# Causal attention: the first group's row maxima computed in two query halves

## The reference, cut to what matters

```python
qkv = (_ln(x, g1, be1) @ w_qkv + b_qkv).reshape(b, t, 3, h, dh)
...
k = jnp.concatenate([k_self, k_ctx], axis=1)
v = jnp.concatenate([v_self, v_ctx], axis=1)
scores = jnp.einsum('bthd,bshd->bhts', q, k) * scale
mask = (j >= t) | (j <= i)
scores = jnp.where(mask, scores, -jnp.inf)
attn = jax.nn.softmax(scores, axis=-1)
attn_out = jnp.einsum('bhts,bshd->bthd', attn, v).reshape(b, t, d)
```

## Time and profile before

| | us |
|---|---|
| median of 3 runs | 1572.62 (1569.34 to 1581.99) |
| the profiled execution, its own time | 1575.25 |
| its span | 1573.5 |
| stage `at0` in that span | about 80 to 429 |

### The profile page before, as it was taken

One profiled execution on the slowest core, in us unless ns is written; L12 is line 12 of the kernel. 1 busy time (PEld: TensorE's weight loads), 2 busy tenths in 40 slices (PEclk: granted clock), 3 DMA queues, 4 the chain that ended last, 5 costly groups with the idle time before them and its releaser, 6 DMA issues.

```text
span 1573.5 us, 21716 instructions
## 1 busy us (share of the span) xinstructions
PE 1345.9 (86%) x7242; PEld 767.7 (49%) x7242; DVE 1071.8 (68%) x2665; ACT 748.6 (48%) x1048; POOL 531.0 (34%) x448
## 2 busy tenths in 40 slices
PE   5869998999779979788998988799998688788896
PEld 4413333333268856544443355444443577545796
DVE  4577777777564367666577768675668888676654
ACT  5405555555867445522334434323343634245664
POOL 3001111111241043205777622078765357001312
PEclk9959999999999999988999989799999979699999
DMA  7952333330000001554313305724400030730001
GB/s 254 264 114 47 58 58 57 58 58 2 14 14 1 1 1 42 157 165 94 79 35 76 113 17 165 212 62 94 95 28 1 27 35 22 161 64 3 1 1 54
DMA packets 79848, 110.29 MB, mean 70 GB/s; under 512 B 16575, under 2 KB 55673, under 8 KB 77945
## 3 DMA queue, kind: packets, MB, share of 16 engines
q1 hardware_dynamic: 79737, 108.91, 27.9%
HBM read 70.55 MB, written 37.80 MB: 69 GB/s over the span
## 4 chain that ended last, share of the span: by engine, by line
PE 42%; DVE 18%; POOLq 15%; issue 10%; ACT 6%; DVEq 3%; DMA 3%; SPq 2%; POOL 1%; ACTq 0%
POOLq L1080 15%; PE banks L1191 6%; PE banks L1551 5%; PE banks L1133 5%; PE banks L1536 5%; PE banks L2096 3%; DVE max_parts L1365 3%; PE banks L1166 3%; PE banks L2122 2%; DVE mask_rows L1361 2%; DVE scratch L1361 2%; PE banks L1144 1%; PE banks L2640 1%; DMA stacks<-neg_max_parts 1%; PE banks L571 1%
## 5 line engine op out<-in xcount | busy, mean ns | idle before, releaser
L1326 ACT ACTIVATE x_feat<-banks,key_bias 128x1024 f32<-128x1024 f32 x160 | 176.5, 1114 | 268.4 <-PE banks L1173 210.4
L1079 POOL TENSOR_TENSOR x_feat<-x_feat 128x1024 f32<-128x1024 f32 (+1 forms) x112 | 243.0, 2170 | 98.7 <-ACT x_feat L1326 90.7
L1133 PE MATMUL banks<-stacks 128*128 128x512 f32 (+4 forms) x640 | 230.6, 408 | 39.9 <-DVE max_parts L1354 14.4
L1191 PE MATMUL banks<-x_feat,v_group 128*32 128x512 f32 (+4 forms) x1312 | 231.6, 570 | 8.7 <-ACT x_feat L1326 4.8
L1326 ACT ACTIVATE x_feat<-banks 128x1024 f32<-128x1024 f32 (+2 forms) x224 | 178.9, 840 | 121.9 <-PE banks L1166 120.1
L1133 PEld LDWEIGHTS banks<-stacks 96*128 96x128 bf16 (+1 forms) x640 | 77.7, 139 | 230.7 <-DVE max_parts L1354 92.9
L1166 PE MATMUL banks<-stacks 99*128 99x512 bf16 (+3 forms) x512 | 132.8, 348 | 23.5 <-ACT x_feat L1326 13.3
L1103 POOL TENSOR_SCALAR_AFFINE_SELECT x_feat<-x_feat 128x256 f32<-128x256 f32 x128 | 53.9, 422 | 289.2 <-ACT x_feat L1326 287.9
L1354 DVE CUSTOM_DVE_ANT_0 scratch<-banks,mask_rows 128x512 f32<-128x512 f32 x128 | 88.2, 689 | 50.2 <-PE banks L1133 50.1
L1172 PE MATMUL banks<-stacks 128*128 128x512 f32 x256 | 111.2, 435 | 9.5 <-DMA stacks<-neg_max_parts_r 9.5
L1536 PE MATMUL banks<-stacks 128*128 128x512 f32 x384 | 101.8, 404 | 9.8 <-DVE stacks L1518 8.9
(11 more groups left out here) (295 smaller groups left out, 2471.4 us busy)
## 6 DMA issues: line engine op xcount, KB each, us to landing
stacks<-q_parts_r SPq DMA_DIRECT2D x18, 512.0 KB, 12.3
stacks<-k_parts_r SPq DMA_DIRECT2D x18, 512.0 KB, 14.1
q_parts_r<-stacks SPq DMA_DIRECT2D x16, 512.0 KB, 3.5
k_parts_r<-stacks SPq DMA_DIRECT2D x16, 512.0 KB, 3.3
v_group<-v SPq DMA_DIRECT2D x14, 512.0 KB, 14.7
stacks<-q_parts SPq DMA_DIRECT2D x16, 384.0 KB, 5.1
w_even<-in_w SPq DMA_DIRECT2D x4, 1024.0 KB, 6.8
stacks<-q_parts SPq DMA_DIRECT2D x16, 256.0 KB, 5.4
```

The costliest lines, as they stand in the source:

```text
L1079: e.tensor_tensor(total, total, p, ALU.add)
L1133: m = e.matmul(PS[:, bank, at:at + wide], q[0:rows, h, qt * P:(qt + 1) * P], keys[0:rows, h, k0:k0 + wide], start=True, stop=True, skip_gr ...
L1191: m = e.matmul(PS[w * h:w * (h + 1), bank, t.q0:CH], V[:, h, :], PB[:, t.index % 2, h // 2, h % 2, 0:CH - t.q0], start=t.first, stop=t.las ...
L1326: e.activation(dst, PS[:, 2 * (st % 2):2 * (st % 2) + 2, 0:CH - t.q0], ACT.Exp, scale=A.scale, bias=bias).then_inc(s.p_ready, 1)
```

## The change

`A.halved` becomes true for `at0` too. The chunks of a head are put in another order, and the chunk that held query tile 1 (half 0) together with query tile 5 (half 1) becomes two chunks of 256 keys, so that no chunk mixes the halves: 10 chunks per head in place of 9, 47 per group in place of 43. This list holds for all 8 groups; the two-part first round only for group 0. The scratch tile of the masked maximum is taken by the running number of the item and not by the chunk's number.

```diff
-                products = [[(i, 0)] for i in range(3, TB)] + [[(7, 1)], [(0, 0), (2, 0)], [(4, 1), (6, 1)], [(1, 0), (5, 1)]]
+                products = [[(3, 0)], [(0, 0), (2, 0)], [(1, 0)]] + [[(i, 0)] for i in range(4, TB)] + \
+                    [[(7, 1)], [(4, 1), (6, 1)], [(5, 1)]]
             A.chunks += [("self", h, p, 0) for h in range(A.nh) for p in products]
-        A.halved = self_keys and dh == 64
+        A.halved = self_keys
...
-                    m = e.tensor_tensor_reduce(CAUSAL_SCR[i % 2][:, at:at + wide], PS[:, bank, at:at + wide],
+                    m = e.tensor_tensor_reduce(CAUSAL_SCR[n % 2][:, at:at + wide], PS[:, bank, at:at + wide],
```

## The result

The changed kernel takes 1602.08 us at the median (1596.97 to 1606.13), against 1572.58 before: a ratio of 1.0164 with a 95% interval of 1.0134 to 1.0193. It is slower, by 29.5 us. The profiled execution took 1606.13 us with a span of 1604.4; it is the slowest of the four runs.

A forecast was written before the change was run, and what follows sets the result against it. The stage was taken to be bound by a chain through VectorE (chunks, split, rows, first scores). First round 11.2 us plus later groups 4.6 gave 15.8, added to 1572.62: 1588.4 us, range 1573 to 1603.

The forecast's parts named there:

- TensorE rival: TensorE sets the stage's pace, so its earlier start counts: 5.2 us won, 0 to 5 lost later, 1567 to 1573; chance 0.13.
- (a): First round, 19 chunks alone before the first combine: 4.1 us of context chunks and 8.6 of self chunks, to 93.8.
- (b): First round, the first combine, turn and split of maxima on VectorE: 2.3 us as before, to 96.1.
- (d): First round, from TensorE's first score to VectorE's first chunk behind it: 1.5 us, to 106.6.
- (c): First round, sending the first rows in 12 transfers: 7.6 us plus 1.3 to land, first score at 105.1.
- (e): First round, 28 chunks of half 1 beside steps 0 to 2 at 0.714 each: 20.0 us, ends 17 and 22.
- clock rival: TensorE's clock stays low longer, steps 3 to 10 start at 1.2 GHz: 11 us more, 1599; chance 0.10.
- (f): First round, the second combine, turn and split as added work on VectorE: 2.3 us, to 128.9.
- (g): First round, second 12 rows: 9.0 us, mostly covered by steps 3 and 4; 1 to 3 us lost, next chunk 139.4.
- (h): First round, 35 remaining chunks in steps 5 to 10: 24.4 plus 0.9 us, group 1's last maximum at 164.7.
- The later groups: Groups 2 to 7, 4 added handshakes of 0.19 us each: 0.76 us a group, 4.6 over six (0 to 21).
- the rival with the full wait: Later groups, each of 8 narrow chunks costs VectorE 0.44 us: 3.5 us a group, 1605; chance 0.12.

The follow-up runs named there:

- 3-transfer kernel: The two-list kernel with the first half's maxima sent in 3 transfers in place of 12; 1585.62 us, ratio 1.0087.
- two-list kernel: The changed kernel with the new chunk list for group 0 alone, groups 1 to 7 on the old list of 43; 1593.28 us, ratio 1.0107.

## Why the prediction was right, and what was too small

The sign, and the chain through VectorE, were right. The time lies in the range by 0.9 us, and two of the four runs lie above it, so that it was held is in part luck. The forecast of 15.8 us more was about half of the 29.5. By its own terms the forecast reached further than I wrote: the upper bounds, 15 for the first round and 21 for the later groups, add up to 1609 and not to 1600. The chances named for "slower" add up to 0.56 and not to 0.52.

*What bounds.* Right, and shown from both sides: work put into VectorE's wait came out of the period (39.1 to 36.5), and the early start of TensorE, 11.9 us, won nothing. The TensorE rival falls by the same run: with TensorE's work unchanged the period went from 39.1 to 36.5.

*(a), (b), (d).* Right to 0.5 us.

*(c), the first rows.* Right: 12 issues of 0.62 us, score at 104.54 for 105.1, and the 3-transfer kernel shows that what is taken off there comes off the end. The Trainium skill's rule on small transfers ("DMA: Bandwidth & Descriptors", section "Rules for kernel authors"), to put them together, agrees with that trace: 9 issues fewer gave 3.9 us.

*(e), 28 chunks.* This is the term of the first round that was mis-sized: 20.0 us from the first chunk to the second combine, measured 24.9 (106.14 to 130.99), above my upper end of 22. I had priced chunks and left out that TensorE runs the steps' other work in the same order. At 1.2 GHz the 8 products with the values take 1.94 us, and VectorE, with two banks to live on, stands for 1.7 us at each of two such places. The clock rival had this mechanism with a chance of 0.10, and it did happen: 0.50 up to 152.8. It put the price at steps 3 to 10, though. With the clock up beside the chunks 3.7 us of this stretch come back. The rest of the 4.9, about 1, I have no run for. What made the clock fall stays open in part: in three runs it was at 0.50 again behind gaps of 2.8 to 3.4 us that the fillers left, in others it fell with no gap over 0.57 or 1.66 us.

*(f), (g).* The second split is there, 2.3 us. The second rows took 7.37 us to issue, and TensorE's weight load for step 5 waited 0.92 us for them; VectorE's first chunk behind that score is at 143.31, where I had 139.4. All of that lateness is (e)'s.

*(h), 35 chunks.* From that chunk to the combine it took 28.0 us (143.31 to 171.35) where I had 25.3; the clock was low up to 152.8 here too, but no run takes the 2.7 apart. In all 17.8 for 11.2.

*The later groups.* The step that failed most, as it counts six times: 0.19 us for a handshake and so 0.76 a group, measured 1.75. That the split costs and not the order was right (40.5 against 39.1), the size was wrong. I took TensorE's wait for a release as the price. The price is VectorE's: where TensorE is at other work, a narrow chunk in a bank covers less of that time, and it comes to 0.35 to 0.44 us for each of 4 more chunks. My reason for the lower bound was the wrong way round: beside the products with the values I took the hand-over to be hidden, as TensorE is late there anyway, and it is there that the wait grew, from 0.43 to 0.88 us at the place shown. The row that I used for the upper end, 0.44 after the narrow context chunk, was the right size by chance, as it comes from another place, and it counts 4 times and not 8. So the rival with the full wait, 1605, lies nearer to the measured time than my forecast does, but not for its reason: its 3.5 us a group was 1.75, and the first round made up for it.

*Sum.* 6 us are missing in the period and 6.6 in the first round. Together with the forecast 15.8 that is 28.3 us, of 28.6 in the stage and 30.9 between the two traced spans; the medians differ by 29.5.

## What to carry to other kernels

Find the one engine through which the stage's chain runs, and move work into the places where that engine waits; an earlier start of an engine that isn't on the chain wins nothing. Where two engines hand each other work through two buffers, the price of one more hand-over is the time that the shorter piece no longer covers while the other engine is at other work, so don't cut pieces short in a list that runs for every group when only the first needs it. Count transfers by issue: rows sent by head and part cost their issue time one after another, right on the path.

## What the runs showed that I had not expected

TensorE's granted clock fell from 2.4 to 1.2 GHz (1.00 to 0.50) in the midst of matmuls, with no long idle stretch ahead: at about 122.2 in the two-list kernel, at 119.0 in the one with 3 transfers (no gap over 0.57 us since the clock had risen in either), and at about 84 in the kernel before with the filler ahead of the stage (1.66 us at most). In all three TensorE ran chunks that wait for VectorE's banks. With one filler matmul behind each chunk it stayed up (1.00) from 107.4 through the same steps.
